# The order of three VectorE steps within each cycle of the mixing: a single tile's maximum, the zeros, the pair's maximum

## What is computed

```
# layer 0: an 8-way attention per sample mixes the channels, then an fp8-rounded product
agg_w = einsum('bk,koi->boi', att, weight);  out = einsum('boi,bih->boh', agg_w, x) + agg_b
amax = max(abs(x));  inv_scale = max(amax, 1e-12) / 448;  q = (x / inv_scale).astype(float8_e4m3fn)
x = x + q(out) @ q(W0.T) * (x_inv_scale * w_inv_scale) + bias
# layer 1: a grouped convolution of 9 taps, then a product with W1 = (W_q - zero) * scale
x = x + (conv(x) + ctx + bias) @ W1.T + bias1
```

## Time and profile before

| | us |
|---|---|
| time, median of 3 runs | 531.81 |
| the profiled execution: its time | 531.02 |
| the profiled execution: its span, first to last instruction | 528.8 |
| busy in the span: TensorE, VectorE, ScalarE, GpSimd | 508.1, 414.6, 244.4, 59.3 |
| of it, TensorE busy with 3460 matmuls at a mean granted clock of | 0.994 |

### The profile page before, as it was taken

How to read it: one execution, slowest core, us unless ns; L and a number is a source line. 1 busy time by engine, 2 the same in 40 slices (tenths; PEclk the granted TensorE clock), 3 DMA queues, 4 the chain that set the end, 5 groups by cost and what they waited for, 6 DMA issues and landing times.

```text
span 528.8 us, 9418 instructions
## 1 busy us (share of the span) xinstructions
PE 508.1 (96%) x3460; PEld 282.1 (53%) x3460; DVE 414.6 (78%) x524; ACT 244.4 (46%) x286; POOL 59.3 (11%) x68
## 2 busy tenths in 40 slices
PE   2999999979999999999999999999999999999997
PEld 2544454455555555555555555555555555555563
DVE  7899999966877777777777777777777777777652
ACT  3579987844444444444444444444444444442310
POOL 5276665030000000000000000000000000000000
PEclk9999999979999999999999999999999999999999
DMA  7999671244675666665556565655665666666632
GB/s 239 393 385 408 242 283 42 79 92 131 185 198 168 201 184 177 189 180 180 180 180 180 180 180 180 180 180 180 180 180 180 183 182 184 181 188 185 195 120 79
DMA packets 85650, 100.59 MB, mean 190 GB/s; under 512 B 34468, under 2 KB 67046, under 8 KB 85638
## 3 DMA queue, kind: packets, MB, share of 16 engines
q1 hardware_dynamic: 84610, 99.41, 59.6%
q0 software_dynamic: 656, 0.82, 0.9%
q10 hardware_dynamic: 372, 0.20, 0.2%
HBM read 58.41 MB, written 32.75 MB: 172 GB/s over the span
## 4 chain that ended last, share of the span: by engine, by line
PE 79%; DVE 11%; DMA 4%; issue 2%; SPq 1%; ACT 1%; POOL 1%; DVEq 0%; ACTq 0%; POOLq 0%
PE pair L1167 40%; PE pair L1141 19%; PE pair L1157 16%; DVE stat L804 5%; DMA work<-work 2%; DMA Y<-in_L_ffn_weight_dram 2%; PE pair L1047 1%; PE pair L1131 1%; DVE work L729 1%; DVE work L819 1%; DVE Y L819 1%; SPq L336 1%; DVE work L732 1%; POOL fixed L489 1%; DVE work L741 1%
## 5 line engine op out<-in xcount | busy, mean ns | idle before, releaser
L1167 PE MATMUL pair<-f1T,work 128*128 128x512 f16 x1024 | 231.0, 379 | 0.0
L1167 PEld LDWEIGHTS pair<-f1T,work 128*128 128x128 f16 x1024 | 98.9, 98 | 113.4
L608 ACT ACTIVATE work<-Y,consts 128x1024 bf16 (+1 forms) x29 | 33.3, 1148 | 187.0 <-DVE work L902 187.0
L921 DVE TENSOR_TENSOR work<-Y,work 128x512 f16<-128x512 f16 (+1 forms) x64 | 71.3, 1120 | 47.3 <-ACT work L641 46.2
L1141 PE MATMUL pair<-f0T,work 128*128 128x512 bf16 x464 | 104.9, 379 | 0.7 <-DMA work<-work 0.7
L1157 PEld LDWEIGHTS pair<-taps,work 128*128 128x128 f16 x1536 | 90.4, 99 | 10.0 <-issue 2.7
L1157 PE MATMUL pair<-taps,work 128*128 128x128 f16 x1536 | 93.0, 221 | 2.6 <-DMA work<-work 2.6
L934 DVE TENSOR_TENSOR Y<-pair,Y 128x512 f32 (+1 forms) x64 | 44.1, 689 | 44.9 <-PE pair L1167 44.9
L641 ACT CAST work<-Y 128x512 f16 (+1 forms) x64 | 69.7, 1138 | 18.5 <-DVE Y L911 15.6
L1141 PEld LDWEIGHTS pair<-f0T,work 128*128 128x128 bf16 x464 | 45.3, 98 | 55.7 <-DMA work<-work 1.2
L1047 PE MATMUL pair<-Y,work 128*128 128x512 f32 x128 | 62.6, 625 | 1.2 <-DVE work L792 0.8
(11 more groups left out here) (153 smaller groups left out, 229.9 us busy)
## 6 DMA issues: line engine op xcount, KB each, us to landing
Y<-in_x_dram SPq DMA_DIRECT2D x64, 512.0 KB, 3.9
out_dram<-Y SPq DMA_DIRECT2D x31, 512.0 KB, 3.8
split_rows<-work SPq DMA_DIRECT2D x30, 520.0 KB, 2.6
work<-split_rows SPq DMA_DIRECT2D x30, 520.0 KB, 3.9
Y<-in_L_ffn_weight_dram SPq DMA_DIRECT2D x8, 512.0 KB, 5.7
Y<-in_L_ffn_W_q_dram SPq DMA_DIRECT2D x5, 512.0 KB, 13.2
work<-in_L_ffn_W_q_dram SPq DMA_DIRECT2D x3, 512.0 KB, 15.5
work<-work SPq DMA_DIRECT2D x8, 65.0 KB, 3.8
```

The costliest lines, as they stand in the source:

```text
L921: nc.vector.tensor_tensor(split[:, r, s, 1], v[:, r, :], split[:, r, s, 0], ALU.subtract)\
L1167: last = mm(ps[2 + h][:, :], y1s[n][:, e, k, :], f1T[:, k, h * H:(h + 1) * H], start=False, stop=(e == 1 and k == KT - 1), skip_group_chec ...
```

## The change

The pair and the single change places in the table of groups, and `less_w1(r)` moves from ahead of the maxima to between them. A cycle of VectorE was: offset of layer 0's piece, zeros, pair (tiles 3r+1 and 3r+2), single (3r+3). It is now: offset, single (3r+1), zeros, pair (3r+2 and 3r+3). In cycle 0 tile 0's maximum takes the single's place ahead of the zeros, and the maxima of tile 1 and of tiles 2 and 3 follow. Number and shapes of the instructions are the same.

```
-        groups = [(0, 1)] + [g for r in range(R8) for g in ((3 * r + 1, 2), (3 * r + 3, 1))]
+        groups = [(0, 1)] + [g for r in range(R8) for g in ((3 * r + 1, 1), (3 * r + 2, 2))]
...
                 round_offset(dve, w0f[:, r, :], wz[r % 2], w_mul, w_chain, 3 * r)
+                if r == 0:
+                    largest_mixed(0)
+                else:
+                    largest_mixed(2 * r + 1)
                 less_w1(r)
                 if r == 0:
-                    largest_mixed(0)
-                largest_mixed(2 * r + 1)
+                    largest_mixed(1)
                 largest_mixed(2 * r + 2)
```

## The result

The changed kernel took 535.12 us (median of 12 runs, 533.79 to 539.0) beside 529.93 us for the kernel before in the same series. The ratio is 1.0092 with a 95% interval of 1.0074 to 1.0111: slower by a little less than 1%. The forecast was 535.8 us, in a range of 531.5 to 539.

What follows compares the result with a forecast made beforehand. VectorE's chain was taken to set the pace of the mixing, 7.07 us a cycle. Terms of +0.94, +2.64, +0.94 and -0.56 us sum to +3.96 on a median of 531.81: 535.8 us, range 531.5 to 539.

Steps and rivals of the forecast that it cites:

- The pace of the mixing: From 25 to 78 us VectorE sets the pace, 7.07 us a cycle with no idle time in between.
- What holds whom: VectorE and GpSimd: less_w1 held L489; after the change L489 holds less_w1, and L729's hold of 0.50 us goes.
- The size of the hold: less_w1 in each of eight cycles waits for the rest of L489, 0.94 us, with L489's work taken as 2.0 us.
- The sum: VectorE up to tile 31: +0.94 in cycle 0, 2.64 in cycles 1 to 6, +0.94 in cycle 7, -0.56; +3.96 us.
- the waits that went: VectorE's last maxima, tiles 30 and 31: the wait of 0.56 us for ScalarE goes, since VectorE arrives late.
- SyncE's queue and TensorE: Later less_w1 delays loads; TensorE waits 1.3 us for tile 20, about 0.8 more for tile 21; cost 0.
- the cover: TensorE waits for L489 of cycle 7 anyway, with about 1 us to spare, so late loads cost nothing.
- `less_w1` passes GpSimd: Rival: GpSimd first does not hold less_w1; a cycle is 6.57 us, the time 531.5 us; chance 0.09.
- nothing is held: Rival: L489 really works 3 us; only tile 3's wait, +0.5 us, counts, giving 532.3 us; chance 0.05.
- The fallen clock: Rival: TensorE's clock falls behind the maxima, +6 to +8 us, 538 to 540 us; chance 0.12.
- the longer stand-still: TensorE's wait ahead of the turn of the maxima grows from 0.96 to 2.4 us, the clock rival's cause.

Runs made afterwards that it cites:

- e3: The changed kernel with GpSimd's L489 (round_w0) done on half of the columns only: 530.30 us, ratio 0.9987 to the kernel before.
- e4: The kernel before with the same half of GpSimd's L489 (round_w0) left out: 530.36 us, ratio 0.9992.
- e2: The kernel before with its old table of groups, but less_w1 between the pair and the single: 534.05 us, ratio 1.0065.
- e5: The changed kernel with twelve of TensorE's narrow sums ahead of the wait for the maxima, in place of five: 537.44 us, ratio 1.0129.
- e7: The changed kernel itself, measured again: 535.97 us, ratio 1.0107 to the kernel before.
- e12: The changed kernel with matmuls of no use in three TensorE gaps, eight ahead of the maxima's turn, four and ten later: 533.70 us, ratio 1.0057.
- e8: The changed kernel, but GpSimd starts L489 only when less_w1 of the same cycle is through: 540.92 us, ratio 1.0205.
- e10: The kernel before with matmuls of no use in three TensorE gaps, four ahead of the maxima's turn, four and ten later: 528.32 us, ratio 0.9947.
- e11: The kernel before with matmuls of no use in the two late TensorE gaps only, four and ten: 528.33 us, ratio 0.9944.
- e9: The changed kernel with eight matmuls of no use in TensorE's gap ahead of the maxima's turn only: 534.85 us, ratio 1.0084.

## Why the prediction was right, and where its sizes were off

*The pace of the mixing.* Right: VectorE's list and its holds set it, and the end of the last maximum moved by 5.0 us, nearly the whole difference of 5.2.

*What holds whom.* Right in all three parts: L489 has 2.1 us of its own work and was held by `less_w1`; in the new order `less_w1` is held by L489 as L729 had been by L483; L729 is free. That a two-input instruction of VectorE is held by GpSimd had no row before; now the one at 45.41 us has it, 2.32 us long, and e3 shows the hold shrink with L489. This agrees with the rule of the Trainium skill, "SBUF — State Buffer", section "Who interferes with whom", by which whichever issues first keeps the other out.

*The size of the hold* is the term that was mis-sized. I took L489's work from the distance between the end of `less_w1` and its own, 2.0 us. It is 2.13. My reading is that a part of it, its start-up, goes by unseen while L489 is held; e3 and e4 have the same with half the work, 1.16 us free and 1.01 behind a hold. So the hold is 1.02 us in cycles 0 and 1 and 1.09 to 1.11 from cycle 2 on, not 0.94, and a cycle 7.68 us, not 7.51.

*The sum*, from cycle 0's L734 to the last maximum, as measured: cycle 0 +1.02 (0.94 predicted), cycle 1 +0.53 and cycles 2 to 5 +0.61 each, together 2.97 (2.20), cycle 6 +0.79 (0.44), and from there to the end +0.23 (0.94 - 0.56 = 0.38). That makes 5.0 where I had 4.0. Cycle 6 is special: L483 starts 0.37 us late there, so that L729 is held once more (0.60 us); e2 and e5 show it too, and I don't know why. At the end the waits that went were worth 0.85 us, not the 0.56 of the row: some 0.2 us of waiting ahead of the maximum of tiles 27 and 28 lay hidden in the row of five, and the 0.08 us that neighbours overlap is lost at a wait. That the forecast for the median nevertheless lies close (535.8 and 535.1) is partly luck: the three runs of before had a median 1.9 us above that of the twelve, and on the latter my sum would have given 533.9.

*SyncE's queue and TensorE.* Right. TensorE waited 1.73 us for tile 20 (1.3 predicted) and 0.80 for tile 21 (0.8), and then still 1.04 us for L489 of cycle 7 (about 1): the cover held, though that turn came 3.7 us later than before, at 85.27, where I had 2.6. The cover is thin, though. In e7's profile TensorE waited 2.66 us for tile 20, in e12's 1.64 for tile 20 and 2.23 for tile 21, and in neither was a wait for L489 left. Loads that land later still would move the end, as the prediction says; whether that made some of the long executions is not shown.

*The rivals.* That `less_w1` passes GpSimd, and that nothing is held, are both refuted by 2.32 and 2.13 us. The fallen clock was real: in the profiled execution it cost about 4 us, and its 539.0 us lie within that rival's 538 to 540. Two more of the twelve, at 537.09 and 537.74 us, had a mean clock of 0.987, but no profile shows where. It did not reach the median. Its cause as I gave it, the longer stand-still of 2.05 us (2.4 predicted), was not confirmed by e5.

## What to carry to other kernels

Where VectorE and GpSimd work beside each other, write down for each instruction whether the other engine can run beside it, and put those that cannot so that the long one of the slower engine does not start just ahead of a VectorE instruction that everything waits for. Here the order zeros, pair, single was good since VectorE's two such instructions followed each other directly, and GpSimd's instruction took the wait, where it cost next to nothing (TensorE waited 0.22 us for it, once). By the rows here VectorE's maxima run beside GpSimd at their full pace (1.21 us beside L489), while `less_w1`, L729 and, in e8, L732 (L733 there) are held, although the last two read one tensor only. An instruction's recorded length can contain a wait: an end that keeps a constant distance to another engine's end gives it away, but the work read from that distance is too short by the start-up.

Where TensorE stands still ahead of a dense stretch, matmuls of no use in that gap are worth a try: in gaps of 1.0 and 2.57 us they brought 2.0 us by the medians here (ratio 0.9944). In the early gap they brought nothing that can be told.

## What the runs showed that I had not expected

The clock fell ahead of the first convolution in every profile without the late fillers, and fourteen matmuls of 0.22 us prevented it in the profiles of e10, e11 and e12, worth 2.0 us of 530; the mean clocks of e11's eleven executions, 0.997 to 1.000, say the same. The early fall at 96 to 99 us comes in some executions of either order (e3, e5, e7, the changed kernel, and e10 on the old order), whether the stand-still there is 2.05 us (the changed kernel), 1.64 (e7), 0.96 (e3), 0.54 (e5) or at most 0.16 at a time (e10). In other profiles the clock also fell while the tiles were still being mixed: in e4 at 24 us behind a stand-still of 2.17 us, in e7 at 67 us behind one of 2.66, in e8 at 53 us behind one of 1.77.

A GpSimd instruction that has to wait for VectorE in cycle 6 starts 0.37 us later than in any other cycle (1.60 us of idle time instead of 1.23) in the changed kernel, e2, e5, e7, e9 and e12. In e8 it is L490 that starts 0.38 us late in that cycle. In e3, which has one GpSimd instruction more ahead of it, there is no such delay. No experiment followed this.
